# Mamba layer with a top-2 mixture of experts: expert slots rotated by one tile, and one 128-row tile per expert computed ahead of the rest

## The reference

```python
x = layernorm(x + mamba(x))           # 256 inner channels, 16 states, a scan over 1024 tokens
logits = x @ w_g                      # 2048 tokens, 8 experts
topv, topi = top_k(logits, 2)
probs = softmax(all but the two set to -1e9)
capacity = int(2 * 1.25 * 2048 / 8)   # 640 rows per expert
rank = cumsum over (first choices of all tokens, then second choices) per expert, minus 1
mask = mask * (rank < capacity)       # rows past 640 are dropped
h = gelu(rows_of_expert @ c_fc[e])    # (640,128) @ (128,512)
exp_out = h @ c_proj[e]               # (640,512) @ (512,128)
out = sum over both choices of weight * exp_out
x = layernorm(x + out)
```

## Times and profile before

| | |
|---|---|
| three runs | 379.13, 380.09, 380.87 us, median 380.09 |
| the profiled execution | 379.31 us, of which its span is 377.6 |
| PE, DVE, POOL, ACT busy | 289.0, 283.8, 264.7, 220.5 us |
| PE busy from 263 to 273 us | 0.0 us |
| PE busy from 285 to 355 us | 70.0 us |

### The profile page before, as it was taken

The page is one execution under the profiler, slowest core; times in us unless marked ns, Lnnn a source line. Parts: engine busy times, 40 slices in busy tenths (PEclk is TensorE's granted clock), DMA queues, the critical chain, the costliest instruction groups (busy, mean ns, idle before and its releaser), DMA issues. The chain is left out here.

```text
span 377.6 us, 5742 instructions
## 1 busy us (share of the span) xinstructions
PE 289.0 (77%) x1795; PEld 221.6 (59%) x1795; DVE 283.8 (75%) x448; ACT 220.5 (58%) x450; POOL 264.7 (70%) x224
## 2 busy tenths in 40 slices
PE   8797899677877739967564899775089999999900
PEld 6445456455765425757452564333089999999900
DVE  2699889999999799999889899996213444444655
ACT  1858987969965695776767665852203333333405
POOL 4607589977898799978989997896623555555532
PEclk9999999999999997968986799999589999999965
DMA  7061078564354254212112231001151434435773
GB/s 225 17 226 57 2 216 270 183 168 158 85 174 131 92 155 146 91 63 99 69 58 78 92 112 56 0 15 42 36 147 38 132 110 119 119 90 155 212 193 112
DMA packets 35693, 42.87 MB, mean 114 GB/s; under 512 B 3830, under 2 KB 26235, under 8 KB 35664
## 3 DMA queue, kind: packets, MB, share of 16 engines
q1 hardware_dynamic: 32240, 37.32, 32.4%
q0 software_dynamic: 2304, 4.24, 3.4%
q10 hardware_dynamic: 1120, 0.97, 0.8%
HBM read 30.11 MB, written 12.79 MB: 114 GB/s over the span
## 5 line engine op out<-in xcount | busy, mean ns | idle before, releaser
L1451 POOL TENSOR_TENSOR product<-state,c_wide 128x1024 f32<-128x1024 f32 x64 | 149.9, 2346 | 38.1 <-DVE state L1690 25.4
L1073 ACT ACTIVATE psum<-dt,a_neg 128x512 f32<-128x512 f32 x86 | 57.6, 684 | 32.6 <-DVE state L1690 31.2
L689 PE MATMUL psum<-ident,product 128*128 128x128 f32 x384 | 53.3, 285 | 17.4 <-POOL product L1451 17.4
L1690 DVE TENSOR_TENSOR_SCAN state<-psum,drive 128x512 f32<-128x512 f32 x50 | 59.7, 1212 | 4.3 <-ACT psum L1073 4.1
L689 PEld LDWEIGHTS psum<-ident,product 128*128 128x128 f32 x384 | 45.4, 147 | 27.6 <-POOL product L1451 24.0
L1661 DVE TENSOR_TENSOR drive<-dtu,psum 128x1024 f32<-128x1024 f32 x45 | 54.0, 1200 | 3.6 <-PE psum L656 3.6
L1575 POOL DMA_INDIRECT result_rows<-state,result_at x30 | 31.2, 1040 | 35.3 <-DVE state L1912 24.5
L1690 DVE TENSOR_TENSOR_SCAN state<-psum,carry,drive 128x512 f32<-128x512 f32 x40 | 50.4, 1270 | 0.2
L1912 DVE TENSOR_SCALAR state<-psum,result_weight 128x128 f32<-128x128 f32 x40 | 14.1, 351 | 38.9 <-PE psum L953 29.7
L940 PE MATMUL psum<-product,fc_sb 128*128 128x128 f32 x320 | 42.3, 275 | 1.1 <-DVE product L1872 1.1
L1532 POOL DMA_INDIRECT slot_rows<-sent,scatter_at x32 | 32.8, 1025 | 10.3 <-issue 6.8
(11 more groups left out here) (258 smaller groups left out, 541.2 us busy)
## 6 DMA issues: line engine op xcount, KB each, us to landing
c_wide<-c_rows SPq DMA_DIRECT2D x32, 512.0 KB, 4.1
slot_rows<-blank SPq DMA_DIRECT2D x8, 325.0 KB, 4.8
c_wide<-slot_rows SPq DMA_DIRECT2D x8, 325.0 KB, 3.7
result_rows<-zeros SPq DMA_DIRECT2D x8, 256.0 KB, 5.0
late_rows<-zeros SPq DMA_DIRECT2D x8, 256.0 KB
fc_sb<-in_c_fc SPq DMA_DIRECT2D x8, 256.0 KB
proj_sb<-in_c_proj SPq DMA_DIRECT2D x8, 256.0 KB
c_wide<-result_rows SPq DMA_DIRECT2D x8, 256.0 KB
```

The lines of the kernel that those rows point to most:

```text
L689: last = nc.tensor.matmul(y_part(j, d), product[:, i, d, j * P:(j + 1) * P], ident[:, :], is_transpose=True, start=False, stop=True, skip_ ...
L1073: nc.scalar.activation(psum[:, A_BANK + d, :], dt[:, q % 2, d, :], ACT.Exp, scale=a_neg[:, n:n + 1]).then_inc(decay_ready, 1)
L1451: nc.gpsimd.tensor_tensor(product[:, U % PRODUCTS, channels, :], state[:, U % RING, channels, :], wide, ALU.mult).then_inc(product_ready, 1)
L1690: nc.vector.tensor_tensor_scan(state[:, U % RING, d, :], decay, rows, before, ALU.mult, ALU.add).then_inc(scanned, 1)
```

## The change

An expert's 640 slots are rotated by one tile of 128. First choices now start at slot 128 and wrap round at 640 into slots 0 to 127; second choices start at slot 127 and go down, then wrap to 639. The earliest first choices and the earliest second choices therefore lie side by side. After three chunks the kernel counts each expert's first choices so far (`count_early`, seven small instructions on DVE between the last product and the last gate), and starts from min(count, 128) to find 128 neighbouring rows, which it loads and computes before the last chunk's rows are there ("early" tiles). Those 128 slots are missing from the expert's later work: the late rows are the other four tiles, and of the first two loaded tiles a mask (`mask_rows`) keeps, lane by lane, the row that was not early; PE adds the two turned tiles together. Where fewer than 128 rows are there, the second choices of the last chunk skip the empty places. Empty slots now hold 0 in place of a far row number, which the row numbers take up by an offset (`NOWHERE`).

Where the weights go: experts 0 and 1 in a buffer of their own, 2 to 7 in `x_tok`, `z_tok` and half of `u`, which are free by then. All eight are loaded during the scan. Core of the diff:

```diff
 # SP
-            for e in range(2, N_EXP):
-                sp.wait_ge(fc_done, SLOT_TILES * (e - 1))
-                load_first(e // 2, e % 2)
...
-                sp.wait_ge(proj_done, SLOT_TILES * (e - 1))
-                load_second(e // 2, e % 2)
...
+                if m in (20, 22):
+                    sp.wait_ge(x_turned, NQ)
+                    load_weights(2 + (m - 20) // 2)
+                if m in (29, 30):
...
+                    load_weights(4 + m - 29)
+                if m == 31:
+                    sp.wait_ge(dtu_ready, DT * NQ)
+                    sp.wait_ge(summed, DT * ((NQ - 1) * D_STATE + 1))
+                    load_weights(6)
+                    load_weights(7)
+            sp.wait_ge(early_found, 1)
+            starts = [sp.value_load(early_from[0:1, e:e + 1], min_val=e * CAPACITY, max_val=e * CAPACITY + P) for e in range(N_EXP)]
+            sp.wait_ge(seconds_sent, 16 * (TILES - TPC))
+            sp.wait_ge(firsts_sent, 16 * (TILES - TPC))
...
+            for e in range(N_EXP):
+                sp.dma_start(early_rows[:, e, :], slot_rows[bass.ds(starts[e], P), :]).then_inc(early_loaded[e // 2], 16)
             sp.wait_ge(seconds_sent, 16 * TILES)
             sp.wait_ge(firsts_sent, 16 * TILES)
 # PE
+            nc.tensor.matmul(psum[:, B_BANK + 1, 0:TOP_K * N_EXP], ones[:, :], marks[:, 0:TOP_K, :, 0], start=True, stop=True).then_inc(early_counted, 1)
             add_to_y(LAST - 1)
...
+            warm(16)
             pe.wait_ge(x1_ready, TILES)
             pe.wait_ge(ranks_taken, NQ)
-            pe.wait_ge(seconds_sent, 16 * (TILES - TPC))
-            pe.wait_ge(firsts_sent, 16 * TILES)
-            for _ in range(26):
-                nc.tensor.matmul(psum[:, 2, 0:P], ident[:, :], ident[:, :], start=True, stop=True)
...
+            pe.wait_ge(weights_loaded, 16 * 2 * N_EXP)
+            turn_early(0)
+            first_product(0)
+            for k in range(FFN_TILES):
+                if k + 1 < FFN_TILES:
+                    first_product(k + 1)
+                if k in (0, 2, 4):
+                    turn_early(1 + k // 2)
+                if k == N_EXP - 2:
+                    turn_rows(0)
+                second_product(k)
+                if k == N_EXP - 1:
+                    turn_rows(1)
+                if k >= N_EXP:
+                    e, s = divmod(k - N_EXP, LATE_TILES)
+                    if s == LATE_TILES - 1 and e + 2 < N_EXP:
+                        turn_rows(e + 2)
 # DVE, in place(q)
+                nc.vector.tensor_tensor(wraps[:, :, :], rank_of(q)[:, 0:TOP_K, :], wrap_from[:, :, :].to_broadcast([P, TOP_K, TPC]), ALU.is_ge
...
+                chain(nc.vector.scalar_tensor_tensor(slot_base[:, :, :], wraps[:, :, :], -float(CAPACITY), slot_base[:, :, :], ALU.mult, ALU.add))
+            def count_early():
+                dve.wait_ge(early_counted, 1)
...
+            def mask_rows(e):
...
+                nc.vector.tensor_tensor(both, both, swap[:, e, :].unsqueeze(2).to_broadcast([P, 2, ROW]), ALU.mult).then_inc(rows_masked, 1)
 # DVE, after the routing of the last chunk
-            for e in range(2):
-                center_proj(e)
-                copy_turned(e)
+            center_proj(0)
+            copy_early(0)
+            center_proj(1)
+            copy_early(1)
+            for e in range(N_EXP):
+                if e + 2 < N_EXP:
+                    center_proj(e + 2)
+                if e in (2, 4):
+                    copy_early(1 + e // 2)
+                if e == 4:
+                    tag_early()
+                if e == N_EXP - 2:
+                    mask_rows(0)
+                    copy_turned(0)
+                if e == N_EXP - 1:
+                    mask_rows(1)
+                take_early(e)
+            copy_turned(1)
...
-                for g in [(0,), (1,), (2, 3), (), ()][s]:
+                for g in [(0,), (1, 2), (3,), ()][s]:
                     add_first(g)
-                for g in [(), (), (), (0, 1), (2, 3)][s]:
+                for g in [(), (), (0,), (1, 2)][s]:
                     add_second(g)
 # POOL, behind the last chunk's scatters
+            for e in range(N_EXP):
+                send_early(e)
```

288 lines of the change are left out of this document (183 added, 105 removed).

## The result

The changed kernel takes 376.63 us (median of 14 runs, 373.73 to 380.56) beside 379.85 for the kernel before (14 runs): ratio 0.990, interval 0.987 to 0.992. The forecast was 369.0, with a range from 366.3 to 373.5. The ratio leaves out two slow runs, those more than 1.5% above the fastest. The profiled execution took 374.95, 4.4 less than that of before; its span is 373.0, 4.6 less. The forecast had 10.8. The runs spread over 1.8%, those of before over 0.6%.

A forecast was written before the change was run, and what follows sets the result against it. Bound: PE's expert-stage work behind a wait for rows (11.22 us idle). Gain 11.7 - 0.6 (scan) - 0.3 (end) = 10.8 takes the profiled 379.31 to 368.5, median 369.3, given as 369.0 us; range 366.3 to 373.5.

The forecast's parts named there:

- When the early tiles can start: Start of expert stage: chunk 2's last scatter lands at 264.2, first early rows at 267.0, first product at about 268.1.
- X: Start of the first late product, before at 282.96: PE allows 282.7, rows 284.6, DVE 284.45; taken as 284.7.
- the two microseconds more that the prediction works out for scatters blocked in full: DVE/GpSimd port lock at full length: five subtractions delay the scatters 3.5 us, X about 286.7; not taken.
- 65 products and 7 turns, 61.9: PE's work left after the first late product: 65 x 0.893 + 3.85 = 61.9 us, before 75.3.
- PE ends at X + 61.9: End of PE's expert work: 346.6 in place of 358.3, 11.7 us earlier.
- PE should then run without a hole: Sign for the late stage: from near 285 PE runs unbroken to about 347.2; holes there mean the forecast is wrong.
- Loads of weights, scan, SP's reads of addresses: Weight loads moved into the scan cost nothing; scan costs 0.6 us; SP's eight address reads are hidden up to 1.04 us each.
- rival 4: SP's eight address reads ahead of early loads are dear: loss begins at 1.04 us each, slower from 2.3; chance 0.05.
- The end, 0.3: Result loads and last take at the kernel's end give back 0.3 us, bounds 0 and 2.
- Rival 3: End gives back 2 us: result and late loads queue, last take waits for an add lacking rows; 371, chance 0.09.
- The sum: Whole kernel: gain 11.7 - 0.6 - 0.3 = 10.8 us, profiled execution 368.5, median given as 369.0.

The follow-up runs named there:

- b_tail_apart: Changed kernel with the four loads of expert 6's late results held until expert 7's last scatter has landed, on chip 6: 372.62 us.
- groups a, c, d and e: Follow-up runs on chips 4 (a), 14 (c and d) and 15 (e); the changed kernel took 376.57, 379.50 and 379.27 us in a, c, d and did not run in e.
- group b: Four edits of the changed kernel on chip 6, without the changed kernel itself: 370.57, 370.23, 370.49 and 372.62 us.
- b_paced: Changed kernel with early results' targets computed two tiles earlier and each early scatter held until two more tiles are done, on chip 6: 370.49 us.
- c_tail_apart: Changed kernel with expert 6's late result loads held until expert 7's last scatter has landed, on chip 14: 377.47 us.
- a_late_start: Changed kernel with the early loads held till all rows are scattered, so the overlap is gone, on chip 4: 391.15 us.
- e_pause_all: Changed kernel, early targets two tiles earlier, 0.5 us POOL memset ahead of early and first eight late scatters and between the last chunk's, chip 15: 383.08 us.
- c_nosend: Changed kernel without the eight scatters of the early results (those output rows are missing), on chip 14: 371.99 us.
- c_paced: Changed kernel with early targets computed two tiles earlier and each early scatter held until two more tiles are done, on chip 14: 373.27 us.
- a_nocenter: Changed kernel with the experts' second weights not centered (reduction and subtraction replaced by a one-element copy), on chip 4: 378.71 us.
- d_paced: Changed kernel with early targets two tiles earlier and each early scatter held until two more tiles are done, chip 14 again: 375.18 us.
- d_paced_closer: Changed kernel with early targets two tiles earlier, each early scatter waiting for one more tile instead of two, on chip 14: 375.34 us.

## Why the prediction was wrong

**When the early tiles can start**: nearly right. The first turn was forecast at 267.6 (with the 0.6 of the scan) and came at 268.62. Chunk 2's last scatter took 3.0 us to land, not 2.3.

**X**: on chip 6 it came out: 285.25 in b_tail_apart against 284.7 and 0.6, and 284.70, 285.41 and 286.45 in the other three (in the last one DVE waited 0.5 us for the late rows). The scatters of 1.2 to 1.4 us beside subtractions are there too. In the changed kernel it was wrong by 2.1 us, and this is the first step that failed: each term took a semaphore for seen as soon as the instruction ended. What ended last was DVE's chain, not the rows: the last scatter was issued at 277.60, where near 277 was forecast, expert 0's rows landed at 283.4, and DVE masked them at 285.00, having come there late by its waits for PE's updates (1.26 us ahead of the take at 276.44). So the two microseconds more that the prediction works out for scatters blocked in full (X near 286.7) are not what the 287.39 show: the scatters were not that late. Three chained waits of DVE in the routing (0.30, 0.36, 0.53) belong to the same picture: one to three like them are in every trace of groups a, c, d and e, and none in the four of group b.

**65 products and 7 turns, 61.9**: "PE ends at X + 61.9" is the step that failed next, by 2.4: "PE should then run without a hole" did not hold, which the prediction had named as a sign of being wrong. The changed kernel has 64.6 by PE's modelled end, and each trace of chip 6 has 62.3. PE has no slack in this stage, and a product that is not reported for 4 us stops ACT, then DVE, then PE.

**Loads of weights, scan, SP's reads of addresses**: the scan is 0.6 longer, as forecast (last product of POOL at 255.65 for 255.07). The eight reads take 0.26 to 0.47 us each, start 0.60 apart and end at 260.9, where a loss would have begun at 1.04 a read, so rival 4 had no ground. The clock stayed at 1.00 over PE's 2.42 us. In seven other traces it was at about 0.50 from 264 to 266, during the identity products, but back at 1.00 before the first early product.

**The end, 0.3**: mis-sized, it measured 2.0 in the changed kernel's first trace and 1.3 to 1.7 in its three others. Rival 3 had the size, 2 us, but not the way: the last take comes 0.5 us behind PE's modelled end, as before. It is the last scatter, which lands 2 us later beside the late loads. Those used to be asked for 2.9 us ahead of PE's end, and their last packet ended at 361.42, 1.1 behind the issue of that scatter at 360.33. Now they are asked for 0.4 behind PE's end, and their packets move for nearly the whole of its 4.4 us. They start later because the scatter that they wait for, expert 6's last, is issued one tile nearer to PE's end and takes 5.6 us in place of 4.1 to land.

**The sum** on chip 6: PE's end 11.06 earlier in b_tail_apart (forecast 11.1) and 9.9 to 11.6 over the four traces, tail 1.7 longer in b_paced. The changed kernel itself did not run on that chip. From b_tail_apart, less the 2.0 that it pays in the tail, it would be at 370.6; an estimate, in the range. Most of what I took from the trace of before was right; that it could not show how this kernel's engines are told of each other's work in a stretch where nothing waits was what I missed. Of the shortfall in the profile 4.5 us go with late updates and 1.7 with the tail.

**The spread** of 1.8% is not explained. b_tail_apart spans 0.2% over 4 runs and c_tail_apart, the same kernel on chip 14, 1.6%; but two other kernels on chip 6 span 1.0%, with one run of four 3 us above the rest, and a_late_start spans 0.2% with late updates in its trace. So why the median lies 1.7 over the profiled run, where the forecast had added 0.8, is not shown either.

**Not settled**: what in a chip makes it one or the other kind, and by which path POOL's issuing delays other engines' updates. All runs carry a recorded span; whether an unrecorded execution has the late updates is not known.

The version that beats both on chip 14 is b_paced: 373.27 and 375.18 there, where the changed kernel took 379.5 and 379.3 and the kernel before 379.7, a gain of about 1.3% (intervals 0.981 to 0.993 and 0.983 to 0.991). On chip 6 it took 370.49.

## What to carry to other kernels

Work that is moved under another engine's burst inherits what the burst does to everything beside it. A stretch in which everyone waits shows nothing of that, so a duration read there is a lower bound. Spread a backlog of scatters over the tiles that make it, rather than let it wait and run off in a row. Before believing a difference of 1 to 2%, run the yardstick in the same group: here the same kernel stood 5 us apart on two chips, while the kernel before did not move.

## What the runs showed of the hardware

- Scatters issued by POOL in a row with 0.30 us between them go with semaphore updates of PE up to 5.4 us late (e_pause_all), on three of four chips. With the 0.40 to 1.44 of the kernel before, or 0.68 to 1.43 in c_nosend, none was late. It takes a few: in c_paced the row begins at 294.04 and the first late update is at 297.5.
- When the row ends, what was held comes in a bunch, in the changed kernel five updates within 0.35 us, 1.2 us behind the end of the row's last scatter.
- A scatter of 128 rows lands 2.3 us after its issue alone (b_tail_apart, c_tail_apart), 4.4 us beside four loads of 256 KB and 5.6 us beside eight (changed kernel).
- In one hole of 4.16 us PE's clock went from 1.00 to 0.50 (a_nocenter); behind holes of 2.85 and 3.06 it was at 0.50 and 0.52 (d_paced, d_paced_closer); over 2.42 us it did not move.
